# Six of eight token groups routed through two sorted sets, the first of them inside the second attention

## The reference

```
hidden_after_attn = hidden_states + proj_out
ln2_out = _layernorm(hidden_after_attn, ln2_weight, ln2_bias)
x = ln2_out.reshape(-1, H)                       # 4096 tokens of 128
gate = softmax(x @ router_weight.T)              # 8 experts
top_probs, top_idx = top_k(gate, 2)
h_mid = gelu(x @ moe_w1[e]);  expert_out = h_mid @ moe_w2[e]   # F = 256
return hidden_after_attn + sum over the two chosen e of prob_e * expert_out_e
```

## Time and profile before

| | us |
|---|---|
| median of 3 runs (lowest, highest) | 858.46 (857.76, 860.21) |
| the profiled execution | 858.81 |
| its span, first to last instruction | 857.1 |
| PE busy | 682.1 (80%) |
| DVE busy | 618.1 (72%) |
| ACT busy | 396.1 (46%) |
| POOL busy | 272.6 (32%) |
| mean granted clock of TensorE | 0.924 of 2.4 GHz |

### The profile page before, as it was taken

One profiled execution on the slowest core, in us unless ns is written; L12 is line 12 of the kernel. 1 busy time (PEld: TensorE's weight loads), 2 busy tenths in 40 slices (PEclk: granted clock), 3 DMA queues, 4 the chain that ended last, 5 costly groups with the idle time before them and its releaser, 6 DMA issues. The chain is left out here.

```text
span 857.1 us, 25305 instructions
## 1 busy us (share of the span) xinstructions
PE 682.1 (80%) x9852; PEld 508.4 (59%) x9852; DVE 618.1 (72%) x1708; ACT 396.1 (46%) x822; POOL 272.6 (32%) x415
## 2 busy tenths in 40 slices
PE   3468979888788898889999477887877997987790
PEld 2345655555556676677788235665665875766680
DVE  7568877887867888989998476887765689633324
ACT  3022333322244565656756355665644774444440
POOL 3333122332425123321100453334013225724660
PEclk9969999999897999999999679999998999999995
DMA  4000000041035211222110000000007400243115
GB/s 104 10 13 22 23 21 21 23 95 21 14 95 115 79 55 45 69 79 82 56 37 12 9 2 4 5 5 3 5 5 122 4 15 25 67 109 83 44 47 163
DMA packets 55173, 38.76 MB, mean 45 GB/s; under 512 B 16332, under 2 KB 50840, under 8 KB 55064
## 3 DMA queue, kind: packets, MB, share of 16 engines
q1 hardware_dynamic: 49720, 31.49, 15.4%
q0 software_dynamic: 2304, 4.76, 1.6%
q10 hardware_dynamic: 3040, 0.98, 0.5%
HBM read 18.27 MB, written 14.75 MB: 39 GB/s over the span
## 5 line engine op out<-in xcount | busy, mean ns | idle before, releaser
L984 ACT ACTIVATE P<-bank 128x512 f32<-128x512 f32 x128 | 76.6, 598 | 75.4 <-PE bank L1130 74.1
L1056 DVE TENSOR_SCALAR bank<-bank 128x512 f32<-128x512 f32 x128 | 88.8, 694 | 16.9 <-PE bank L1121 16.0
L2260 PE MATMUL bank<-w2r,hme 128*128 128x128 f32 (+1 forms) x672 | 94.3, 285 | 3.7 <-DVE Xq L2075 2.9
L2260 PEld LDWEIGHTS bank<-w2r,hme 128*128 128x128 f32 x672 | 87.7, 198 | 13.8 <-ACT hme L2033 5.4
L1064 DVE TENSOR_REDUCE mx<-bank 128x4 f32<-128x512 f32 x128 | 86.9, 680 | 0.7 <-PE bank L1104 0.6
L500 ACT ACTIVATE w2r<-bank 128x512 f32<-128x512 f32 x40 | 23.9, 597 | 113.5 <-PE bank L814 78.8
L2033 ACT ACTIVATE hme<-bank,b 128x512 f32<-128x512 f32 x64 | 43.6, 686 | 47.3 <-PE bank L97 47.2
L1130 PE MATMUL bank<-mT,negsel 128*128 128x128 f16 x512 | 51.0, 223 | 13.5 <-DVE bank L1056 12.1
L973 POOL TENSOR_TENSOR inv_sum<-inv_sum,dn 128x16 f32<-128x16 f32 x32 | 7.0, 219 | 164.8 <-DVE dn L1085 147.1
L2075 DVE SCALAR_TENSOR_TENSOR Xq<-bank,wgte,Xq 128x128 f32<-128x128 f32 x128 | 36.0, 344 | 31.0 <-PE bank L2260 30.8
L95 PE MATMUL bank<-xTe,w 128*128 128x128 f16 (+1 forms) x144 | 42.6, 304 | 16.9 <-DVE xTe L2171 9.3
(11 more groups left out here) (454 smaller groups left out, 1914.2 us busy)
## 6 DMA issues: line engine op xcount, KB each, us to landing
cross_q<-qh SPq DMA_DIRECT2D x24, 128.0 KB
Q<-cross_q SPq DMA_DIRECT2D x8, 384.0 KB, 3.9
XS<-sorted_x SPq DMA_DIRECT2D x10, 260.0 KB, 3.0
sorted_x<-zero SPq DMA_DIRECT2D x1, 2560.0 KB, 16.6
X<-in_x SPq DMA_DIRECT2D x8, 256.0 KB, 2.8
Xq<-X SPq DMA_DIRECT2D x32, 64.0 KB
cross_k<-kh SPq DMA_DIRECT2D x16, 128.0 KB
Yq<-Y SPq DMA_DIRECT2D x32, 64.0 KB
```

Of the source, the lines that this page charges most:

```text
L984: act.activation(P[j][:], TB[u % 3][:], ACT.Exp, scale=SCALE).then_inc(s["p_ready"], 1)
L1056: dve.tensor_scalar(TB[(U * b + j) % 3][:], TB[(U * b + j) % 3][:], -CLIP, CLIP, ALU.max, ALU.min).then_inc(s["t_clip"], 1)
L2260: last = pe.matmul(Y[m % 2][:, cols(i)], hm[:, k % HR, cols(i)], w, start=(b == 0 and i == 0), stop=(b == 1), skip_group_check=True)
```

## The change

- Groups 0 to 5 are sparse, in two sets (0, 1, 2) and (3, 4, 5). Each has 12 tiles, is sorted into 32 tiles (`SLOTS` = 2·12 + 8) and computed in 8 items. Groups 6 and 7 are dense. That makes 16 sparse and 16 dense items, in the order: set 0 (8), six items of group 6, set 1 (8), the last two of group 6, eight of group 7.
- The jobs of groups 0 to 5 run inside `attention2`, one a chunk from q = 10 on, placed by `joined(q)`. At k = 2 PE projects and DVE adds; at k = 3 DVE takes the statistics, POOL root and sum, and ACT normalises at the end of its step; at the next k = 0 PE transposes, ACT and DVE make the halves; at k = 1 PE makes the logits and DVE reads them. All of it uses the banks PX and VM.
- `place` of set 0 runs on DVE at q = 22 to 31, its exp on ACT at q = 22, its counting matmuls on PE at q = 26. POOL sends set 0 by 24 scatters listed at q = 27 to 31. `place` of set 1 runs in blocks 0 to 10 of `experts1`, and POOL sends set 1 after root and sum of group 6.
- The two sorted lists are filled with zeros by two transfers at the start of `attention2` (before: two at the start of `experts1`).
- `choose` is taken from the start of an item's first matmuls to the odd block before, ahead of the `down` matmuls there.
- Results are written to DRAM in sorted order by SP (`keep_y`), and POOL fetches them by 24 gathers a set (`back`), two for each tile. Before, they went by scatters and were loaded by SP. `finish` of groups 0 and 1 runs in blocks 52 and 58, that of groups 2 to 5 after the last block. The rows carry no index columns any more, and L2166 and L2168 are gone.

The core of the diff:

```diff
-DENSE, SPARSE = (0, 1, 2, 3), (4, 5, 6, 7)
-STARTS = (None, 0, 4, 7, 12, 16, 24, 28)
-CUT = 29
+SETS, DENSE = ((0, 1, 2), (3, 4, 5)), (6, 7)
+STARTS = {6: 2, 7: 26}
+FINISH = (52, 58)
...
+        FIRST, ROUTED, COUNTED = -12, 22, 26
+        PLACES = {0: (0,), 1: (1,), 2: (2,), 3: (3, 4), 4: (5,), 5: (6,), 6: (7,), 7: (8,), 8: (9,), 9: (10,)}
+        SENDS = {27 + i: range(5 * i, min(5 * i + 5, 2 * NT)) for i in range(5)}
+        def joined(q):
+            n, k = q // 4, q % 4
+            return {0: n - 3, 1: n - 3, 2: n - 2, 3: n - 2}[k] if 0 <= n - (3 if k < 2 else 2) < NSP else None
...
# POOL, attention2
+                    if k == 3 and joined(q) is not None:
+                        expert_root(pool, e, joined(q))
+                        expert_sum(pool, e, Xq, H, joined(q))
+                    if q in SENDS:
+                        expert_send(pool, e, 0, SENDS[q])
# ACT, end of step
+                    if k == 3 and joined(q) is not None:
+                        expert_normalise(act, e, H, joined(q))
+                    if k == 0 and joined(q) is not None:
+                        expert_high(act, e, PX, joined(q))
+                    if q == ROUTED:
+                        place_exp(act, e, 0)
# DVE, after Vq
+                    if k == 3 and joined(q) is not None:
+                        expert_stats(dve, e, H, PX, joined(q), 1)
# DVE, end of step
+                    if g is not None and k == 0:
+                        expert_low(dve, e, PX, g)
+                    elif g is not None and k == 1:
+                        gather_logits(dve, e, LGS, g)
+                    elif g is not None and k == 2:
+                        dve.wait_ge(s["h_ready"], g + 1)
+                        expert_stats(dve, e, H, PX, g, 0)
+                    for p in PLACES.get(q - ROUTED, ()):
+                        place(dve, e, PRE, 0, p)
# PE, before the maxima are added
+                    if g is not None and k == 0:
+                        after(pe, s["xT_lo"], min(n + 2, G))
+                        expert_turn(pe, e, ident, PX, g)
+                    elif g is not None and k == 2:
+                        pe.wait_ge(s["at_f"], n)
+                        pe.wait_ge(s["at_lo"], g + 1)
+                        expert_project(pe, e, AT, wp, PX, g)
# PE, end of step
+                    if k == 1 and joined(q) is not None:
+                        after(pe, s["v_ready"], min(q + 2, QUADS))
+                        expert_logits(pe, e, LGS, joined(q))
...
# experts1, POOL
+                def back(n):
+                    for i in range(4):
+                        pool.wait_ge(y_out[i], 16 * (NU // 4) * (n + 1))
+                    for t in range(NT):
+                        for k in range(2):
+                            pool.indirect_dma_start(
+                                out=ZT[n][:, k, t, :], out_offset=None, in_=e["ys"][n],
+                                in_offset=bass.IndirectOffsetOnAxis(ap=e["pos"][n][:, k, t:t + 1], axis=0)
+                            ).then_inc(z_in[(NT * n + t) // GB], 16)
+                expert_root(pool, e, DENSE[0])
+                expert_sum(pool, e, X3, H, DENSE[0])
+                expert_send(pool, e, 1, range(2 * NT))
+                expert_root(pool, e, DENSE[1])
+                expert_sum(pool, e, X3, H, DENSE[1])
+                back(0)
+                back(1)
# experts1, PE
                 for k in range(BLOCKS):
+                    if k % 2 == 0 and coming(k) is not None:
                         slots_turn(coming(k))
                     up(k)
+                    if k % 2 == 1 and coming(k) is not None:
+                        choose(coming(k))
```

More of the change, by code:

```diff
@@ L1559, in turn @@
                     after(pe, s["at_f"], n - 2)
+                    after(pe, e["s"]["ph_ready"], n - 3)
                     for k in range(4):
@@ new lines, in expert_state @@
+        "r16": keep["expert"]["r16"], "rb": keep["expert"]["rb"], "b1": keep["expert"]["b1"], "ones": keep["ones"],
+        "steps": [0],
+        "xsrc": sb("xsrc", [S, GB * NSP, C]), "zero": sb("zero", [128, C]), "tri": sb("tri", [128, 128]),
+        "before16": sb("before16", [128, NE, NE], F16), "iota8": sb("iota8", [128, NE]),
+        "marks": sb("marks", [128, NT]), "iotaT": sb("iotaT", [128, SLOTS]),
+        "lgs": [sb(f"lgs{i}", [128, NT, NE]) for i in range(2)], "prs": [sb(f"prs{i}", [128, NT, NE]) for i in range(2)],
@@ L1725, in expert_sum, with expert_send, normalised, expert_normalise @@
     pool.tensor_tensor(group(X3, g), group(X3, g), group(H, g), ALU.add).then_inc(e["s"]["r_ready"], 1)
-def expert_high(act, e, ps, j):
+def expert_send(pool, e, n, rows):
+    q = e["q"]
+    pool.wait_ge(q["filled"], 32)
+    for r in rows:
+        k, t = r // NT, r % NT
+        pool.wait_ge(q["pos_ready"], 2 * n + k + 1)
+        pool.indirect_dma_start(out=e["xs"][n], out_offset=bass.IndirectOffsetOnAxis(ap=e["pos"][n][:, k, t:t + 1], axis=0),
+                                in_=e["xsrc"][:, NT * n + t, :], in_offset=None).then_inc(q[f"sent{n}"], 16)
+def normalised(e, g):
+    if g in DENSE:
+        return lambda i: e["xn"][:, i, :]
+    return lambda i: e["xsrc"][:, GB * g + i, :]
+def expert_normalise(act, e, H, g):
+    s, xn = e["s"], normalised(e, g)
+    act.wait_ge(s["rs_e"], g + 1)
+    if g == DENSE[1]:
+        act.wait_ge(s["xT_e_psum"], g)
+    for i in range(GB):
+        last = act.activation(xn(i), group(H, g)[:, i, :], ACT.Identity, bias=e["nb"][:, 1, i:i + 1],
+                              scale=e["rs"][:, 1, i:i + 1])
+    last.then_inc(s["xn_e"], 1)
+def expert_high(act, e, ps, g):
     s = e["s"]
-    act.wait_ge(s["xT_e_psum"], j + 1)
-    act.activation(tok(e["xT"][0], JOBS[j]), ps[:], ACT.Copy).then_inc(s["xTe_hi"], 1)
+    act.wait_ge(s["xT_e_psum"], g + 1)
+    if g < NSP:
+        after(act, s["lg_psum"], g - 1)
+    act.activation(turned(e["xT"][0], g), ps[:], ACT.Copy).then_inc(s["xTe_hi"], 1)
 def expert_exp(act, e, d):
@@ new lines, in experts1 @@
+        e["c8"] = sb("c8e", [128, 3, GB, NE, NE])
+        stage = keep["Yq"][:].rearrange("p n c -> p (n c)")
+        XS = [stage[:, N * i:N * i + N].rearrange("p (i c) -> p i c", c=C) for i in range(4)]
+        YS = [stage[:, N * (4 + i):N * (4 + i) + N] for i in range(4)]
+        xh = [sb(f"xhs{i}", [C, 4 * N], F16) for i in range(2)]
+        ZT = [sb(f"ZT{i}", [S, 2, NT, C]) for i in range(2)]
+        landed = [nc.alloc_semaphore(f"slots_in{i}") for i in range(4)]
+        y_out = [nc.alloc_semaphore(f"y_out{i}") for i in range(4)]
@@ L1913, in jobs @@
+        z_in = [nc.alloc_semaphore(f"z_in{i}") for i in range(NSP)]
+        room.held += landed + y_out + z_in
         def jobs(k, p):
-            return [j for j in range(1, len(JOBS)) if k - STARTS[j] == p]
+            return [g for g in DENSE if k - STARTS[g] == p]
         def item(k):
@@ L2197, in _ @@
                     for p in (4, 3, 2, 0):
[L2198 to L2206 removed]
+                        for g in jobs(k, 7 + p):
+                            expert_gate(dve, e, LG, g, p)
@@ L2208, in _ @@
+                    if k in FINISH:
+                        finish(FINISH.index(k))
+                for g in range(len(FINISH), NSP):
+                    finish(g)
             @block.tensor
```

637 lines of the change are left out of this document (275 added, 362 removed).

## The result

The changed kernel takes 887.07 us (median of 4 runs, 885.49 to 889.64) against 858.11 (857.47 to 860.21) for the kernel before in the same session: ratio 1.0336, 95% interval 1.0305 to 1.0367. It is slower by 29 us. The forecast was 875.0, slower, with a range of 857 to 890, so the sign held and the size was 12 us short. 887 lies in the stated range only because that range was stretched upwards for dearer gathers (rival 3), which did not come; the forecast's own range, 866 to 884, was missed by 3 us. The profiled execution has a span of 883.7 us and a mean granted clock of 0.885.

A forecast was written before the change was run, and what follows sets the result against it. In attention DVE had 2 us left a chunk and no engine was free. Delays put `Vq` of step 27 at 660.9, the first sorted gelu at 706.8, the end at 868.9; 5 for clock gave span 873.9, forecast 875, range 857 to 890.

The forecast's parts named there:

- rival 3: End of the expert stage: gathers of set 1 cost more than scatters, up to 27 us, near 890 for half; chance 0.08.
- The wait at the chunk's end: Attention, after k = 3: `mc` queues behind the normalising on ACT, 4.6 us later each time, 18.4 us for four.
- Rival 1: Attention: idle time takes the 18.4 us wait and its share of the clock, giving 854; chance 0.09.
- The rest of a job: Attention chunks: a job's remaining DVE and PE work costs 2.0 us a chunk, 8.0 for four (bounds 3.6 and 16.4).
- the placing: Attention, q = 22 to 27: `place` of set 0 costs 7.3 us ahead of its scatters (bounds 0 and 12).
- the clock: PE's clock falls in idle time: 5 us, from four attention waits and 2 us at the expert stage's start.
- rival 4: Attention: the clock falls at every wait and stays low for a step, 8 us instead of 3, giving 883; chance 0.08.
- The scatters: Set 0's 24 scatters run back to back at 1.28 us, plus 3.1 for root and sum of group 5: 665.6 to 698.1.
- From scatters to items: After set 0's last scatter: landing 2.4 us, load 3.0, then 3.3 to the first sorted gelu at 706.8.
- The list: Expert stage: sparse items take 5.80 us each, dense items 3.08, with 4 us kept for jobs and `place`.
- Rival 2: Sparse items: the early `choose` hides the value loads, 18 us less, giving 857; chance 0.05.
- rival 5: Expert stage: waits as forecast, but list and jobs gain 15 us more, so no change at 858; chance 0.06.

The follow-up runs named there:

- warm: Changed kernel plus 60 small unused PE matmuls ahead of the half scores in each step k = 0 after a job; 878.27 us, ratio 1.0267.
- pool_norm: Changed kernel with POOL normalising in attention, transposes at the end of k = 0, value loads back at the item's start; 863.25 us, ratio 1.0067.
- late_turn: Changed kernel with normalising moved to k = 0, transposes to the end of k = 1, logits to the end of k = 2; 869.71 us, ratio 1.0148.

## Why the prediction came out as it did

The forecast's span of 873.9 is 9.8 us under the measured 883.7. Split at its own steps:

| stretch | forecast | measured |
|---|---|---|
| to `Vq` of step 27 | 660.9 and 3 of clock = 663.9 | 669.05 |
| from there to the first scatter | 4.7 | 5.5 |
| 24 scatters with root and sum of group 5 | 32.5 | 32.4 |
| last scatter to first sorted gelu | 8.7 and 2 of clock | 13.6 |
| first sorted gelu to the end of the span | 162.1 | 163.2 |

- **The wait at the chunk's end: right in place and near in size.** 4.6 us each and 18.4 for four were forecast; with the small matmuls in the pause the first four steps k = 0 grow by 20.7, and this holds the job's transposes too. That it is ACT's order that makes it is half right: with the normalising behind `mc`, 10 to 13 us of attention come back, and to have the step at 5.5 the transposes have to move too. Rival 1 (idle time takes the wait) fell.
- **The rest of a job, the placing and the clock: the sum's failed terms.** From q = 11 to 27 attention grew by 41.6 us. After 18.4 for the wait, 23 remain, against 8.0 + 7.3 + 3 = 18.3. The placing took 0 to 2 of them, not 7.3, so job and clock took 21 to 23, not 11. The clock, for which I took 0.75 a chunk, is 1.4 to 2.2 in each of the first four steps k = 0 (7.1 in all, by warm). That leaves 14 to 16 for the job's rest and for the clock in the other steps, where I had 8.0. So both terms are near twice the forecast or above it, and the placing, far too dear in the sum, hid 5 to 7 us of that: without this second error the forecast would have been 17 to 19 us short instead of 12. Chunks were forecast at 23 us and took 25 to 29.
- **The clock's part.** The granted clock of the first four chunks is 0.80 to 0.87, with PE idle for over 5 us in each, against 1.00 in the earlier trace rows. The Trainium skill (TensorE: Matmul & The Clock Gate, Part 1) says a TensorE that idles between bursts falls back to half its clock. These rows agree. The prediction's rival 4 (8 us of waits instead of 3) had this term right.
- **The job's part.** The bank `PX` shows in the trace of the changed kernel as a wait of `turn` for the add into H, 1.15 and 0.74 us at the ends of the first two chunks; at k = 1 PE waits 1.02 to 1.06 for `mc` behind the copy of the transposed rows. These are some 2 us a chunk; what the remainder is made of is not shown.
- **The scatters: right** to 0.1 us, and their pitch of 1.26 carries over to the gathers at 1.25 (1.28 forecast). Rival 3 (dearer gathers) fell.
- **From scatters to items: under-sized by 3 us.** "Attention's own rest ends near 700" was wrong. Behind the normalising of group 5 stand `Of`, the reciprocals, `Af` and `AT`, and they end at 710.9. I had followed the root and not what is queued behind it. But this costs less than 1 us: from the last scatter to the load it is 4.2 us here, and still 3.5 (pool_norm) and 3.7 (late_turn) where `AT` ended 2.7 and 3.3 us ahead of the load. So what lies between the last scatter and the load, its landing and the barrier, was under-sized: 2.4 in the sum, 3.5 to 3.7 in these two; the load takes 3.7 instead of 3.0. From the first transposes to the gelu it is 5.7 where 3.3 and 2 of clock were kept; the exp of set 1's placing on ACT, with a table load behind it (1.28 us at 719.23), wasn't in the sum.
- **The list: right by two errors, which is luck.** 96.1 us for the sorted items instead of 92.8, with 3 us for the early loads in set 0 where I had said nothing; and the six dense items between the sets take 20.8 instead of 18.5. Beyond the loads that is 2.6 us for jobs and placing, less than the 4 that I kept. The four `finish` take 9.0 us behind the dense list, as forecast (9.1). Rival 2 (they hide the loads) has the wrong sign, and rival 5 (the list gains 15 us more) fell.
- **The balance.** Attention ends 52 us later (691.6 against 639.2), and what follows is 26 us shorter (192.1 against 217.9). By order, and by POOL normalising instead of ACT, 30 us of the whole come back (887 to 857), and the kernel is where it was: in the best version here six sorted groups gain nothing over four, and both sets still begin when their 24 scatters of 1.26 us are through.

What stays open: how much of the 29 us left in attention is DVE's work and how much the bank `PX`; no kernel here had a bank of its own for the jobs.

## What to carry to other kernels

Work moved into a pipeline that has 2 us of room a chunk can cost its latency and not only its busy time: list, for each of its instructions, what is queued behind it on that engine and which PSUM bank it holds, since moving one instruction may only pass the wait to the next in line. Here it paid to give the normalising to the engine that made its input (POOL), and to put the transposes where the bank was free anyway. A block number in a hand-made list is a due time; whoever reorders the list changes it.

## What the runs showed of the hardware

- 60 small matmuls without use in each of five pauses of PE shortened the step with the pause by 1.0 to 2.2 us, 8.1 in all; the whole time is 0.5% lower (1.0267 against 1.0320), but there the intervals overlap.
- Three dense items that start after PE's long pause spent their first 5 us at a granted clock of 0.50 (1.2 GHz); the first sorted item came 4.6 us later for their 9.2 us.
- An indirect gather costs POOL what a scatter costs: 0.94 us busy, 1.25 from one to the next, against 0.96 and 1.26.
- The place of an item's four value loads among PE's matmuls matters in one set and not in the other: 3 us in the eight items of set 0, beside which jobs and placing run, nothing that shows in set 1.
